# Layer 0's queries and keys: projected with features on the partitions and gathered by head through DRAM

## The reference, cut

```python
qkv = h @ Wqkv                                     # h: 2 x 2048 x 256, Wqkv: 256 x 768
q = qkv[..., :512].reshape(2, 32, 2048, 16)        # a plain reshape of 2048 x 512
k = qkv[..., 512:640].reshape(2, 8, 2048, 16)
v = qkv[..., 640:].reshape(2, 8, 2048, 16)
scores = einsum('bhqd,bhkd->bhqk', q, repeat(k, 4)) / 4     # causal, softmax
aw = softmax(scores); aw = aw[first of each pair] - lam * aw[second of each pair]
attn = aw @ repeat(v, 2)
```

## Time and profile before

| | us |
|---|---|
| median of three runs | 2325.1 (2324.48 to 2326.83) |
| profiled execution, its time | 2326.42 |
| profiled execution, its span | 2324.7 |
| layer 0 attention, about | 0 to 1842 |
| busy in the span: TensorE / VectorE / ScalarE / GpSimd | 2139.5 / 1781.2 / 1578.5 / 677.2 |
| mean granted TensorE clock | 0.944 |

### The profile page before, as it was taken

One profiled execution on the slowest core, in us unless ns is written; L12 is line 12 of the kernel. 1 busy time (PEld: TensorE's weight loads), 2 busy tenths in 40 slices (PEclk: granted clock), 3 DMA queues, 4 the chain that ended last, 5 costly groups with the idle time before them and its releaser, 6 DMA issues. The chain is left out here.

```text
span 2324.7 us, 44417 instructions
## 1 busy us (share of the span) xinstructions
PE 2139.5 (92%) x15852; PEld 879.7 (38%) x15852; DVE 1781.2 (77%) x4535; ACT 1578.5 (68%) x3201; POOL 677.2 (29%) x1203
## 2 busy tenths in 40 slices
PE   7799999999999999999999999999999799889983
PEld 5133333333333323233333333333222288567731
DVE  3888888888888888888888888888887268234477
ACT  2178787878777787878787877778777645245633
POOL 1214141423233242324241423233112134000077
PEclk8599999999999999999999999999999899899955
DMA  5120312112120203030312112120200210000001
GB/s 157 35 57 10 66 20 56 32 43 41 34 49 27 48 31 69 7 69 8 67 21 55 33 42 46 30 49 27 44 2 1 67 35 0 1 1 1 1 27 45
DMA packets 95988, 84.65 MB, mean 36 GB/s; under 512 B 48544, under 2 KB 81440, under 8 KB 95776
## 3 DMA queue, kind: packets, MB, share of 16 engines
q1 hardware_dynamic: 95776, 81.91, 16.0%
HBM read 26.81 MB, written 16.78 MB: 19 GB/s over the span
## 5 line engine op out<-in xcount | busy, mean ns | idle before, releaser
L735 ACT ACTIVATE probs<-b_bank 128x512 f32<-128x512 f32 (+1 forms) x2304 | 1173.7, 577 | 365.7 <-PE b_bank L888 357.6
L606 DVE TENSOR_REDUCE m_part<-a_bank 128x1 f32<-128x512 f32 x1536 | 963.6, 682 | 110.4 <-PE a_bank L872 106.0
L888 PE MATMUL b_bank<-q_pack,k_pack 64*128 64x512 bf16 (+7 forms) x5120 | 921.6, 349 | 18.4 <-ACT probs L735 14.6
L872 PE MATMUL a_bank<-k_pack,q_pack 64*128 64x512 bf16 (+3 forms) x2560 | 814.0, 358 | 60.6 <-DVE m_part L606 30.3
L920 PE MATMUL acc<-probs,v_tile 128*32 128x512 f32 (+3 forms) x5120 | 591.1, 543 | 3.1 <-POOL probs L463 0.8
L603 DVE CUSTOM_DVE_ANT_0 a_bank<-a_bank,mask_a 128x128 f32<-128x128 f32 (+3 forms) x1024 | 479.1, 515 | 130.6 <-PE a_bank L872 128.7
L888 PEld LDWEIGHTS b_bank<-q_pack,k_pack 64*128 64x128 bf16 (+1 forms) x5120 | 289.1, 94 | 550.5 <-ACT probs L735 434.4
L872 PEld LDWEIGHTS a_bank<-k_pack,q_pack 64*128 64x128 bf16 x2560 | 222.4, 94 | 378.3 <-DVE m_part L606 184.0
L463 POOL TENSOR_SCALAR_AFFINE_SELECT probs<-probs 128x512 f32<-128x512 f32 (+1 forms) x192 | 151.6, 789 | 583.2 <-ACT probs L735 583.1
L920 PEld LDWEIGHTS acc<-probs,v_tile 128*32 128x32 f32 x5120 | 108.0, 108 | 192.4 <-issue 122.1
L603 DVE DVE_READ_ACCUMULATOR2_ANT m_part<- 128x1 f32 x1024 | 143.8, 140 | 0.0
(11 more groups left out here) (193 smaller groups left out, 1857.5 us busy)
## 6 DMA issues: line engine op xcount, KB each, us to landing
q_pack<-part SPq DMA_DIRECT2D x384, 64.0 KB, 2.3
k_pack<-part SPq DMA_DIRECT2D x192, 64.0 KB, 2.3
scratch<-qkv_row SPq DMA_DIRECT2D x16, 512.0 KB, 2.8
heads<-scratch SPq DMA_DIRECT2D x16, 512.0 KB, 3.6
xg<-in_L_attn_x SPq DMA_DIRECT2D x16, 256.0 KB, 2.6
scratch<-qkv_row SPq DMA_DIRECT2D x32, 128.0 KB, 2.7
q_pack<-m_rows SPq DMA_DIRECT2D x256, 2.0 KB
x<-in_L_attn_x SPq DMA_DIRECT2D x4, 1024.0 KB, 11.8
```

What stands on the lines that cost most here:

```text
L606: dve.tensor_reduce(out, bank[:, 0:w], AX.X, ALU.max).then_inc(a_maxed, 1)
L735: act.activation(probs[:, n % P_RING, h, at:C], b_bank[bank_no(("B", n, h))][:, at:C], ACT.Exp, scale=HD ** -0.5) \
L872: pe.matmul(a_bank[at % A_RING][:, 0:w], q_pack[buf][rows, hp, 0, q:q + P], k_pack[buf][rows, 0, C * c:C * c + w], start=True, stop=True). ...
L888: ins = pe.matmul(b_bank[bank_no(slot)][:, at:at + C - q], k_pack[par][rows, n2, P * kt:P * (kt + 1)], q_pack[par][rows, h // 2, n2, C * j ...
```

## The change

Queries and keys are now projected with the features on the partitions: `wqkv` is the loaded operand and the rows of `x` are the 256 columns. The tile `qkvT` then holds for each of 512 query features and 128 key features its 256 rows, and only the values (w = 5) are still projected the old way, in two halves. SP writes `qkvT` to `scratch` and reads it back by head in five DMAs straight into `headT`, in runs of 64 numbers (256 bytes), 512 runs a DMA. `headT` then has its columns in the order (block, row), where the order of positions is (row, block), and all readers of `headT` go through `by_position`, which steps by 64 numbers. `heads`, `heads_by_j`, `gather_heads`, `turn_heads`, `take_heads` and the slots T are gone. `first_part` is now eight pieces, at the end of the steps 18 to 25; `split` follows at 19 to 26, and its second operation is a copy from `rest` where it was a subtraction. In the opening the gather of group 1 stands behind `pack(0)`. `TENSOR_TIME` and with it the spread of the units changes slightly.

```diff
-PREP_AT = {4: ("N", 0), **{6 + w: ("W", w) for w in range(WPARTS)}, **{17 + k: ("T", k) for k in range(4)}}
-NORMALISE_AT, DEVIATION_AT, CENTRE_AT, GATHER_AT = 0, 1, 3, 14
+PREP_AT = {4: ("N", 0), **{6 + w: ("W", w) for w in range(WPARTS)}}
+NORMALISE_AT, DEVIATION_AT, CENTRE_AT = 0, 1, 3
 PIECES = 8
-SPLIT_AT = range(22, 22 + PIECES)
+FIRST_AT = range(18, 18 + PIECES)
+SPLIT_AT = range(19, 19 + PIECES)
+ROUND_AT = PIECES // 2
-TENSOR_TIME = {"N": 0.75, "W": 1.26, "T": 0.77, "O": 0.80}
+TENSOR_TIME = {"N": 0.75, "W": 1.16, "O": 0.80}
...
+HEAD_DMAS = QH + 1
+BLOCKS = 2 * D // HD
...
+        def by_position(i, pieces):
+            rows = S // BLOCKS // pieces
+            return headT[0:80, :].rearrange("q (b r) -> q r b", b=BLOCKS)[:, rows * i:rows * (i + 1), :]
+
+        def piece(tile, i, pieces):
+            return tile[0:80, S // pieces * i:S // pieces * (i + 1)].rearrange("q (r b) -> q r b", b=BLOCKS)
...
+                sp.dma_start(q.rearrange("(c p r) -> p c r", c=4, p=P), qkvT[:, 0:4, :]).then_inc(rows_out, 16)
+                sp.dma_start(k.rearrange("(p r) -> p r", p=P), qkvT[:, 4, :]).then_inc(rows_out, 16)
+                sp.dma_start(v.rearrange("(r p e) -> p r e", r=2, p=P), qkvT[:, 5, :].rearrange("p (r e) -> p r e", r=2)) \
+                    .then_inc(rows_out, 16)
+
+            def heads_from_dram(n, buf):
+                sp.wait_ge(rows_out, 48 * (n + 1))
+                if n:
+                    sp.wait_ge(parts_ready, n)
                 q, k, _ = regions(buf)
-                sp.dma_start(heads[:, 0:QH, :], q.rearrange("(h p e) -> p h e", h=QH, p=P)).then_inc(heads_in, 16)
-                sp.dma_start(heads[:, QH, :], k.rearrange("(p e) -> p e", p=P)).then_inc(heads_in, 16)
+                by_head = q.rearrange("(b e h r) -> e b h r", b=BLOCKS, e=HD, h=QH)
+                for h in range(QH):
+                    sp.dma_start(headT[HD * h:HD * (h + 1), :].rearrange("e (b r) -> e b r", b=BLOCKS), by_head[:, :, h, :]) \
+                        .then_inc(heads_in, 16)
+                sp.dma_start(headT[HD * QH:HD * (QH + 1), :].rearrange("e (a b r) -> e a b r", a=QH, b=BLOCKS // QH),
+                             k.rearrange("(b e a r) -> e a b r", b=BLOCKS // QH, e=HD, a=QH)).then_inc(heads_in, 16)
...
             rows_to_dram(0, 0)
-            heads_from_dram(0, 0, None)
+            heads_from_dram(0, 0)
             rows_to_dram(1, 1)
-            heads_from_dram(1, 1, 1)
             sp.wait_ge(pool_consts, POOL_CONSTS)
             pack(0, 0, None)
+            heads_from_dram(1, 1)
             maxima_rows(1, 0, 0)
...
+            def split(n, i):
+                pool.wait_ge(part0_ready, PIECES * n + i + 1)
                 if i == 0:
-                    pool.wait_ge(part0_ready, n + 1)
-                    if n:
-                        pool.wait_ge(packs_in, 16 * PACK_DMAS * n)
-                pool.tensor_tensor(rest[0:80, cols], headT[0:80, cols], part[0][0:80, cols], ALU.subtract).then_inc(rest_ready, 1)
-                pool.tensor_tensor(part[1][0:80, cols], headT[0:80, cols], part[0][0:80, cols], ALU.subtract).then_inc(rest_ready, 1)
-                pool.wait_ge(rest_ready, rest_count(n, i))
-                ins = pool.tensor_tensor(part[2][0:80, cols], rest[0:80, cols], part[1][0:80, cols], ALU.subtract)
+                    pool.wait_ge(packs_in, 16 * PACK_DMAS * n)
+                pool.tensor_tensor(piece(rest, i, PIECES), by_position(i, PIECES), piece(part[0], i, PIECES), ALU.subtract) \
+                    .then_inc(rest_ready, 1)
+                pool.wait_ge(rest_ready, rest_count(n, i, 1))
+                pool.tensor_copy(piece(part[1], i, PIECES), piece(rest, i, PIECES)).then_inc(rest_ready, 1)
+                pool.wait_ge(rest_ready, rest_count(n, i, 2))
+                ins = pool.tensor_tensor(piece(part[2], i, PIECES), piece(rest, i, PIECES), piece(part[1], i, PIECES), ALU.subtract)
...
-                act.activation(qkv_row[:, r, a:a + D], bank[:, 0:D], ACT.Copy).then_inc(rows_ready, 1)
+                out, rows = qkvT[:, w, :], bank[:, 0:D]
+                if w == 4:
+                    out, rows = out.rearrange("p (a r) -> p a r", a=QH), rows.rearrange("p (r a) -> p a r", a=QH)
+                act.activation(out, rows, ACT.Copy).then_inc(rows_ready, 1)
+
+            def first_part(n, i):
+                if i == 0:
+                    act.wait_ge(heads_in, 16 * HEAD_DMAS * (n + 1))
+                    if n:
+                        act.wait_ge(packs_in, 16 * PACK_DMAS * n)
+                act.activation(piece(part[0], i, PIECES), by_position(i, PIECES), ACT.Copy).then_inc(part0_ready, 1)
...
+                for r in range(2 if w == 5 else 1):
+                    for k in range(2):
+                        if w < 5:
+                            ins = pe.matmul(bank[:, 0:D], wqkv[:, k, P * w:P * (w + 1)], hT[:, k, :], start=k == 0, stop=k == 1)
+                        else:
+                            ins = pe.matmul(bank[:, P * r:P * (r + 1)], hT[:, k, P * r:P * (r + 1)], wqkv[:, k, 5 * P:6 * P],
+                                            start=k == 0, stop=k == 1)
```

More of the change, by code:

```diff
@@ L136, in uses_at @@
         what, k = PREP_AT[s]
-        out.append((what, {"N": 1, "W": WPARTS, "T": 4}[what] * (g + 2) + k))
+        out.append((what, {"N": 1, "W": WPARTS}[what] * (g + 2) + k))
     return out
@@ L445, in _ @@
                 negate(m)
-            split(1, 0, 1)
-            def gather_heads(n):
-                pool.wait_ge(heads_in, 32 * (n + 1))
-                pool.wait_ge(turned, 4 * n)
-                pool.tensor_copy(heads_by_j[:, :, :, :], heads[:, :, :].rearrange("p h (j d) -> p j h d", d=HD)) \
-                    .then_inc(heads_ready, 1)
+            for i in range(PIECES):
+                split(1, i)
             def mask(n):
@@ L535, in centre @@
                     .then_inc(xhat_ready, 1)
-            def gather_heads(n):
-                dve.wait_ge(heads_in, upto(32 * (n + 1)))
-                if not (isinstance(n, int) and n == 0):
-                    dve.wait_ge(turned, upto(4 * n))
-                dve.tensor_copy(heads_by_j[:, :, :, :], heads[:, :, :].rearrange("p h (j d) -> p j h d", d=HD)) \
-                    .then_inc(heads_ready, 1)
             normalise(0)
@@ L558, in _ @@
             centre(1)
-            gather_heads(0)
-            dve.wait_ge(part0_ready, 1)
-            dve.tensor_tensor(rest[0:80, :], headT[0:80, :], part[0][0:80, :], ALU.subtract).then_inc(rest_ready, 1)
-            dve.tensor_tensor(part[1][0:80, :], headT[0:80, :], part[0][0:80, :], ALU.subtract).then_inc(rest_ready, 1)
-            dve.wait_ge(rest_ready, 2)
-            dve.tensor_tensor(part[2][0:80, :], rest[0:80, :], part[1][0:80, :], ALU.subtract).then_inc(parts_ready, 1)
+            for i in range(ROUND_AT):
+                dve.wait_ge(part0_ready, PIECES // ROUND_AT * (i + 1))
+                dve.tensor_tensor(piece(rest, i, ROUND_AT), by_position(i, ROUND_AT), piece(part[0], i, ROUND_AT), ALU.subtract) \
+                    .then_inc(rest_ready, 1)
+                dve.wait_ge(rest_ready, rest_count(0, i, 1))
+                dve.tensor_copy(piece(part[1], i, ROUND_AT), piece(rest, i, ROUND_AT)).then_inc(rest_ready, 1)
+                dve.wait_ge(rest_ready, rest_count(0, i, 2))
+                ins = dve.tensor_tensor(piece(part[2], i, ROUND_AT), piece(rest, i, ROUND_AT), piece(part[1], i, ROUND_AT), ALU.subtract)
+            ins.then_inc(parts_ready, 1)
             dve.wait_ge(mod_ready, 2)
@@ L718, in _ @@
                     take_rows(n, w, (1 + WPARTS) * n + 2 + w, a_bank[w % A_RING])
-            for k in range(4):
-                take_heads(0, k, N_PRO - 9 + k)
-            first_part(0)
+            for i in range(PIECES):
+                first_part(0, i)
             act.wait_ge(lam_step, 2)
             act.activation(lam[:, 2:4], lam[:, 0:2], ACT.Exp).then_inc(act_consts, 1)
-            take_maxima(0, N_PRO - 5)
-            for k in range(4):
-                take_heads(1, k, N_PRO - 4 + k)
-            first_part(1)
+            take_maxima(0, N_PRO - 1)
+            for i in range(PIECES):
+                first_part(1, i)
             take_maxima(1, N_PRO)
@@ L750, in _ @@
             for n in range(TAIL):
+                g, s = n // STEPS, n % STEPS
                 for h in range(QH):
@@ L761, in _ @@
                         take_rows(k // WPARTS, k % WPARTS, no, bank)
-                    if what == "T":
-                        take_heads(k // 4, k % 4, no, bank)
                     if what == "M":
@@ L767, in _ @@
                         take_rows_of_output(k, no, bank)
-                    if what == "T" and k % 4 == 3:
-                        first_part(k // 4)
+                if g + 2 < GROUPS and s in FIRST_AT:
+                    first_part(g + 2, s - FIRST_AT[0])
         @block.tensor
@@ L845, in _ @@
             emptied("N", 1)
-            for k in range(4):
```

(4 more changed lines are left out.)

66 lines of the change are left out of this document (13 added, 53 removed).

## The result

The changed kernel takes 2292.84 us (median of 4 runs, 2290.76 to 2294.03) against 2325.97 us (4 runs, 2324.48 to 2330.83): the ratio is 0.9853, 95% interval 0.9836 to 0.9870. That is 33.1 us less, where 43.1 were forecast (2325.1 to 2282). The sign is the forecast's and the time lies inside the outer range of 2268 to 2305, but just outside the forecast's own 2274 to 2292; the gain was a quarter short.

A forecast was written before the change was run, and what follows sets the result against it. TensorE was taken to bound the groups: 3.3 - 0.5 - 0.2, 2.6 to 2.7 us a group, 37.5 over 14, plus 5.7 in the opening, from 2326.4 to 2283.2; forecast median 2282 us, range 2274 to 2292.

The forecast's parts named there:

- outer range: Whole kernel: 2268 to 2305 us, taking in the no-charge rival and most of the dear-read rival, leaving out about 2 in 10.
- What bounds the kernel: Sixteen head groups: TensorE sets the pace, busy 104.06 of 108.48 us; VectorE second; work taken from TensorE returns almost whole.
- The comparison with group 14: Steps 11 to 21: 35.98 us against a clean 31.4 without preparation; the 4.6 difference agrees with 4.4 by single rows.
- Removed: In each of 14 groups, four turnings of heads and TensorE's wait for the long rounding go: 3.3 us.
- Turnings: Four T slots a group, each occupying TensorE 0.57 us: 2.3 us removed.
- Long rounding: `first_part` as one 1.91 us ScalarE operation makes TensorE wait 1.04 us a group; that wait was to go.
- ScalarE's pieces: Eight pieces in steps 18 to 25, 0.55 us each (0.38 to 1.0); six charged 0.08 each, 0.5 us a group.
- Rival (2): ScalarE's strided read costs about 0.8 us a piece, losing 2.2 us a group; total 2306 us; chance 0.16.
- rival (3): Pieces dearer still: no group gain from 0.95 us each; at 1.1 us the kernel takes 2338; chance 0.05.
- the spread of the units: Units of maxima spread anew over a group's steps: TensorE waits 0.2 us more for VectorE, bounds 0 and 0.8.
- The opening: Before group 0: packing starts 4.7 us earlier and the lead regains 1 us; sum 5.7 us, bounds 2 and 8.
- GpSimd, DMA, SP: GpSimd's split pieces fit their steps, gathers land by 1044 before step 18, SP's issues fall in idle time: cost 0.

The follow-up runs named there:

- the old list: Changed kernel with only the spread of units over the steps (ENDS) taken from the kernel before, also called the old spread: 2279.98 us, ratio 0.9797.

## Why the prediction was right, and by how much it was off

**What bounds the kernel** held: four turnings, 2.28 us of TensorE by the rows, cost 2.35 us a group when put back, some 0.3 of it as a wait for ScalarE. The comparison with group 14 held, too: its steps 11 to 22 take 31.66 us at full clock (with the old list), where I had worked out 31.4.

**Removed.** Turnings: 2.28 forecast, 2.35 measured. Long rounding: 1.04 forecast from one wait, 0.52 measured when put back alone, perhaps 0.7 with turnings beside it. That term was too large: the wait that I read was that of a chain (an evacuation, then the rounding), and I gave it to its last link.

**ScalarE's pieces.** Taken at 0.55 us with bounds 0.38 and 1.0; they last 0.67. The strided write that I took for a measure, 0.84 ns a number, was near: the strided read costs 1.0 ns. I charged 0.5 us a group, 0.08 in each of six steps; the strided part alone costs 0.47 (0.35 with the new spread), but in two steps and not in six. The size was right, the place was not. The Trainium skill ("SBUF — State Buffer", under "Door 1: The DMA port swizzle") says that single accesses to new lines of 16 bytes pay; these runs agree, 0.41 against 0.67 us, for ScalarE, and for GpSimd 0.67 against 0.82. Rival (2) needed 0.8 us a piece and rival (3) more; neither came.

**The term that was mis-sized: the spread of the units.** The prediction had "The units of maxima are spread anew over the steps; TensorE already waits some 1.9 us a group for VectorE's `m_part`, and with 93.25 us of work in a shorter group it will wait a little more: 0.2 us, bounds 0 and 0.8". The term was 0.85 us, just over its upper bound. Its mechanism was the right one for the larger part: the waits for VectorE grew by 0.6 us, from 2.5 to 3.1. They grew because of the new list and not because the group is shorter, since with the old list they are 2.5 us in a group of 105.90 where they were 2.6 in one of 108.48. The rest, some 0.25 us, was not in the sum at all: a unit is work of TensorE, too, and has its place. Two units a step go beside the scores of heads, a third stands behind them. The old list has 12 such units, the new one 14, and that could have been counted from `schedule()`.

How the miss adds up: 43.2 us were summed, and 24.4 + 6.6 - 3.4 = 27.6 came from the change in the profiled execution (with group 0's share at full clock). Of the 15.6 us between them the spread has (0.85 - 0.2) x 14 = 9.1, and the groups 14 and 15, where I had nothing, 3.4 (about 2.0 at full clock). What was removed less the pieces gave 2.59 and not 2.8 a group, 2.9. The sum itself slipped by 1.1: 3.3 - 0.5 - 0.2 is 2.6, and 14 x 2.6 is 36.4, not 37.5. The opening gave back 0.9. With the old spread the median is 2280, 2 us from the forecast; that it is so near has luck in it, since the kernel before took 2327.6 beside it, 47.6 more, and 43.1 were forecast.

**GpSimd, DMA, SP** were charged nothing, rightly. Gathers issued at 1010.53 in the group shown land in 4.0 us each (median), and ScalarE's only wait for one is that of the opening, 3.0 us in all (2.97 in the timeline above). TensorE's wait for the masks is 0.8 us over the whole execution in both kernels.

**The opening.** Packing 4.3 us earlier, 4.7 forecast. The lead then is 2.3 us shorter (50.21 to 47.87 us from the first scores of units to those of heads), where I had 1: VectorE's waits in it, but for the first, fell from some 2.7 us to 0.6. GpSimd's split of group 1 ended at 105.0, before 107.9, and nobody waited. One part was given back. The lower clock of the lead ends 5.1 us earlier than before, but group 0 starts 6.65 us earlier. Windows at the start of group 0, before (step 0 at 120.19) and after (113.54):

```profile
120.19:122.50 2.31, 2.31 (x24) 2.05 (x20) 2.23 (x11) 2.24 (x5) 1.22 (x2) 0.54 0.62 106
```

```profile
113.54:117.40 3.86, 3.86 (x33) 2.33 (x28) 3.75 (x15) 3.57 (x8) 1.96 (x3) 0.52 0.60 105
```

By the clocks of 0.54 and 0.52 in these windows the low stretch reached some 2.1 us into group 0 and now reaches 3.7 us; group 0 gained 1.04 us where the others gained 1.74. What sets the end of that stretch, no run shows.

**Right for partly the wrong reason.** Of the 32.4 us between the profiled executions some 6 are the stretches at the lower clock that the one before had and the one after had not. The medians seem to share this: of 21 more executions of the kernel before, three with a mean clock of 0.948 to 0.950 took 2319.0 to 2321.4 us and the others, at 0.942 to 0.945, 2325.6 to 2332.5, while all four of the changed kernel have 0.948 to 0.951. Without them the miss would read larger, about 27 for 43.

**Not settled:** the 0.2 us above; why a third unit costs 0.6 us in step 27, 0.9 in step 30 and 1.2 in the steps 29 and 34, and a second between nothing and 0.5 (the steps differ in the width of their scores and of the units, and only the steps 28 and 29 were read line by line); whether the list has to do with how often the clock falls; and the 0.9 us that layer 0's output and layer 1 grew by, in code that the change doesn't touch.

## What to carry to other kernels

When a change takes work out of a step, look at what a planner does with the room: a list made from estimated times may move other work to places where it no longer overlaps, or bunch it where the engine that consumes it falls behind, and the moved work then costs more than the estimate gained. Count how many pieces find a partner before and after, and compare the lengths of single steps and the waits in them, not only the whole group. A wait read in a trace belongs to the whole chain in front of it; its last link, taken alone, may be worth half of it.

## What the runs showed of the hardware

Reading float32 from SBUF with a step of 64 numbers, against reading them in order: ScalarE 0.669 for 0.411 us (256 numbers, 80 partitions, to bfloat16), GpSimd's subtraction 0.820 for 0.669, VectorE's subtraction of 512 numbers 1.012 for 0.682. A unit (two matrix products of 64 rows) placed beside products on the other 64 rows, as the second of its step, lengthened the step by 0.0, 0.3 and 0.5 us (steps 26, 28 and 35); one placed behind them, as the third, by 0.6, 0.9 and 1.2 (steps 27, 30 and 29), with no wait of over 0.15 us for VectorE in any of them. In the steps 6, 8 and 10, with three units each, TensorE waits 0.3 to 0.5 us a step for VectorE; they last 4.1 to 4.3 us, about three times the 1.4 us that a unit takes VectorE. TensorE's granted clock fell to its lower level for 3.41 us (at times 6.8) amid full work none to five times in the 13 steady groups of an execution. Gathers of 2560 runs of 256 bytes in five DMAs land in 4.0 us (median of 80), where 640 runs of 1 KB in two landed in 3.6.
